# Local scores on TensorE: the products with the queries' high part first, for three groups, and one semaphore each for high and low transposes

## The reference, cut to what matters

```python
q = rmsnorm(apply_partial_rope(h @ Wq_c @ Wq_up))            # per head
k_sw = rmsnorm(apply_partial_rope(h @ Wk)); v_sw = h @ Wv    # one key head
ck = rmsnorm(h.reshape(b, nb, M * HID) @ W_comp)             # 64 blocks of 16 tokens
c_out = attend(einsum(q, ck) * scale, blocks that ended before the token, sink, ck)
s = einsum(q, k_sw) * scale
sw_out = attend(CAP * tanh(s / CAP), the last 64 tokens, sink, v_sw)
inter = einsum('btgf,gfi->btgi', c_out + sw_out, Wg)         # 4 groups
x = layernorm(x + inter @ Wo)
x = layernorm(x + x @ ternary(weight).T + bias)
```

## Time and profile before

| | |
|---|---|
| median of 3 runs | 408.3 us (404.14, 408.30, 408.51) |
| the profiled execution's own time | 405.67 us |
| its span, first to last instruction | 403.9 us |
| mean granted TensorE clock | 0.974 |
| TensorE busy | 364.0 us (90%) |
| VectorE, ScalarE, GpSimd busy | 328.0, 293.3, 280.6 us |
| a step from one tile's local scores to the next | 18.2 to 20.4 us |

### The profile page before, as it was taken

The page is one execution under the profiler, slowest core; times in us unless marked ns, Lnnn a source line. Parts: engine busy times, 40 slices in busy tenths (PEclk is TensorE's granted clock), DMA queues, the critical chain, the costliest instruction groups (busy, mean ns, idle before and its releaser), DMA issues. The chain is left out here.

```text
span 403.9 us, 8848 instructions
## 1 busy us (share of the span) xinstructions
PE 364.0 (90%) x3111; PEld 294.8 (73%) x3111; DVE 328.0 (81%) x676; ACT 293.3 (73%) x833; POOL 280.6 (69%) x197
## 2 busy tenths in 40 slices
PE   6998899779988989999999999988999999989881
PEld 5996678566767778786869787867686868677871
DVE  3688988577989899898989897989898989892524
ACT  4669747768696969797969695978879696958410
POOL 1860155456787888889887977797979797885812
PEclk9999699959999999999999999999999999999997
DMA  8994005498867676758585968686668876676350
GB/s 255 289 268 159 1 0 106 209 262 130 125 98 127 97 132 93 144 80 145 85 152 70 147 98 139 86 145 105 119 120 117 131 116 123 104 127 105 52 86 26
DMA packets 150284, 50.21 MB, mean 124 GB/s; under 512 B 138592, under 2 KB 148832, under 8 KB 149984
## 3 DMA queue, kind: packets, MB, share of 16 engines
q1 hardware_dynamic: 149424, 49.32, 65.3%
q10 hardware_dynamic: 816, 0.33, 0.3%
HBM read 11.87 MB, written 4.19 MB: 40 GB/s over the span
## 5 line engine op out<-in xcount | busy, mean ns | idle before, releaser
L1326 POOL TENSOR_TENSOR room_wg<-room_comp,keep 128x1024 f32<-128x1024 f32 x32 | 75.4, 2355 | 38.4 <-ACT room_comp L868 33.5
L1316 POOL TENSOR_TENSOR ao<-room_wg,ao 128x1024 f16<-128x1024 f32 x31 | 66.2, 2136 | 13.9 <-ACT ao L727 13.8
L687 PE MATMUL PS<-V,room_wg 128*128 128x129 f32 x512 | 67.2, 286 | 5.5 <-POOL room_wg L1326 5.0
L880 ACT ACTIVATE room_h<-PS,room_K 128x8 f32<-128x8 f32 (+7 forms) x256 | 70.8, 392 | 0.5 <-DVE room_K L1129 0.4
L687 PEld LDWEIGHTS PS<-V,room_wg 128*128 128x128 f32 x512 | 62.3, 198 | 9.9 <-POOL room_wg L1326 8.7
L880 ACT ACTIVATION_READ_ACCUMULATOR room_h<-PS,room_K 128x1 f32 x256 | 65.5, 278 | 0.0
L647 PE MATMUL PS<-Weff,aoT 128*128 128x256 f16 x512 | 60.8, 273 | 3.1 <-DMA aoT<-ao 3.0
L1333 POOL TENSOR_TENSOR ny<-nx,nu 128x16 f32<-128x16 f32 x16 | 46.8, 2923 | 20.6 <-DVE o_inv L1095 13.2
L647 PEld LDWEIGHTS PS<-Weff,aoT 128*128 128x128 f16 x512 | 49.6, 98 | 11.7 <-DMA aoT<-ao 5.0
L603 PE MATMUL PS<-room_h,kT 128*128 128x512 f16 x192 | 47.0, 380 | 11.6 <-DMA room_h<-room_K 10.4
L1044 DVE TENSOR_REDUCE ssq<-room_wg 128x8 f32<-128x1024 f32 x30 | 36.5, 1220 | 14.4 <-ACT room_wg L785 14.0
(11 more groups left out here) (186 smaller groups left out, 726.1 us busy)
## 6 DMA issues: line engine op xcount, KB each, us to landing
H<-in_L_attn_h SPq DMA_DIRECT2D x4, 512.0 KB, 6.2
room_wg<-in_L_attn_Wg SPq DMA_DIRECT2D x1, 2048.0 KB, 16.3
cw_rows<-staged SPq DMA_DIRECT2D x1, 2048.0 KB, 6.9
CW<-cw_rows SPq DMA_DIRECT2D x1, 2048.0 KB, 8.0
aoT<-ao SPq DMA_TRANSPOSE x128, 2.7
out<-room_wo SPq DMA_DIRECT2D x16, 128.0 KB, 2.1
CW<-in_L_attn_Wq_up SPq DMA_DIRECT2D x2, 512.0 KB, 9.6
room_wo<-in_L_attn_Wo SPq DMA_DIRECT2D x1, 1024.0 KB, 18.0
```

The lines of the kernel that those rows point to most:

```text
L687: last = nc.tensor.matmul(pv, Pm[:, c, 2 * pr:2 * pr + 2, :], V[:, 2 * i + c, :], start=True, stop=True)
L880: last = nc.scalar.activation(Ec[:, 0:n, hd], bank(4 + hd // 8)[:, (hd % 8) * n:(hd % 8 + 1) * n], ACT.Exp, bias=mn[:, hd:hd + 1], accum_o ...
L1316: G.tensor_tensor(ao16[:, 1, c, :, :], ao[:, c, :, :], ao16[:, 0, c, :, :], ALU.subtract).then_inc(g_al, 1)
L1326: G.tensor_tensor(Pm[:, c, :, :], E[:, c, :, :], keep[:, :, :], ALU.mult).then_inc(g_mask, 1)
```

## The change

For the groups 0 to 2 the products with the queries' high part are all made first (six products, two per group), then the three with the low part; group 3 follows with its three products as before. The high transposes now count on `s_qh` and the low ones on `s_ql`, 32 per tile each. TensorE waits for `s_qh` before the first product and for `s_ql` before the seventh. `norm_T` stands behind the low product of group 1. The two other waits on `s_qt` (ScalarE before it writes a high part again, VectorE before it writes a low part again) now name the semaphore of their own part; each still waits for the tile before. The order in which SyncE issues is the same.

```diff
-                                 transpose=True).then_inc(s_qt, 16)
+                                 transpose=True).then_inc(s_qh if n == 0 else s_ql, 16)
...
-                    pe.wait_ge(s_qt, 64 * i + 64)
                     at = i * P + (i // TPB) * WIN
-                    for u, b in enumerate((6, 4, 5, 6)):
-                        wait(pe, *((a_tanh, 4 * i + 1) if u == 3 else (d_ao, 2 * i)))
+
+                    def local_scores(u, parts):
+
                         c, hf = divmod(u, 2)
-                        for n, (kp, qp) in enumerate(PARTS):
-                            last = nc.tensor.matmul(bank(b), kT[:, kp, at + c * WIN:at + c * WIN + P],
+                        for kp, qp in parts:
+                            last = nc.tensor.matmul(bank((6, 4, 5, 6)[u]), kT[:, kp, at + c * WIN:at + c * WIN + P],
                                                     qT[:, qp, 8 * hf:8 * hf + 8, c * WIN:(c + 1) * WIN],
-                                                    start=n == 0, stop=n == 2)
-                        last.then_inc(p_sw, 1)
+                                                    start=kp == qp == 0, stop=qp == 1)
+                        return last
+
+                    pe.wait_ge(s_qh, 32 * i + 32)
+                    wait(pe, d_ao, 2 * i)
+                    for u in range(3):
+                        local_scores(u, PARTS[:2])
+                    pe.wait_ge(s_ql, 32 * i + 32)
+                    for u in range(3):
+                        local_scores(u, PARTS[2:]).then_inc(p_sw, 1)
                         if ffn and u == 1:
                             norm_T()
+                    pe.wait_ge(a_tanh, 4 * i + 1)
+                    local_scores(3, PARTS).then_inc(p_sw, 1)
...
-                wait(act, s_qt, 64 * t - 48 + 16 * hf)
+                wait(act, s_qh, 32 * t - 16 + 16 * hf)
...
-                    wait(dve, s_qt, 64 * i + 48 + 16 * hf)
+                    wait(dve, s_ql, 32 * i + 16 + 16 * hf)
```

More of the change, by code:

```diff
@@ L210, in build @@
             "g_mask", "g_cn", "g_al", "g_rl", "g_x1", "g_xb", "g_sh"))
-        s_out, s_qt, s_ah, s_al = sem("s_out"), sem("s_qt"), sem("s_ah"), sem("s_al")
+        s_out, s_qh, s_ql, s_ah, s_al = sem("s_out"), sem("s_qh"), sem("s_ql"), sem("s_ah"), sem("s_al")
         s_chain = sem("s_chain")
```

## The result

| | before | changed |
|---|---|---|
| median | 406.58 us (403.4 to 408.88, 20 runs) | 404.92 us (402.94 to 406.78, 20 runs) |
| profiled execution, its span | 405.67, 403.9 us | 406.64, 404.8 us |

The ratio is 0.995 with an interval of 0.9927 to 0.9972: the changed kernel is faster by some 2 us (1.1 to 3.0), where +0.3 us was forecast. The time lies within the forecast range, but it moved by more than its uncertainty, and not in the direction forecast. Two repeats gave 0.9962 (0.993 to 0.9995) and 0.9958 (0.9924 to 0.9992). Every ratio here leaves out the few runs that lie over 1.5% above the fastest of their kernel. The profiled execution of the change is longer than that of before, 406.64 against 405.67 us. This says already that one trace against one trace can't tell where the 2 us are.

A forecast was written before the change was run, and what follows sets the result against it. TensorE is busiest (90%), but ScalarE's row of work from the division's end was taken to set each step. Terms: +0.68 + 0.26 - 0.66 = +0.3 us on the median of 408.3, giving 408.6 us; range 404.0 to 411.0.

The forecast's parts named there:

- The wait removed: Before the local scores: TensorE starts at the division's end, saving 0.42 of 1.09 us of waiting in step 10.
- the first group: Group 0 is released after seven products instead of three: 1.79 us from first product to tanh, before 0.92.
- steps 1 to 6 and 9 to 14: Tanh 1.87 us behind the division, 0.08 us to spare; TensorE's gain is waited out at group 3: worth zero.
- Rival A: TensorE's gain at the front of the steps is passed on: 4.9 us faster, 403.4 us; chance 0.11.
- rival B: Tanh of group 0 in twelve steps lacks the 0.08 us to spare: 1.6 us more, 410.2 us; chance 0.2.
- Steps 7 and 8: TensorE arrives last, ScalarE waits 0.15 and 0.28 us; with step 6's 0.04, less 0.21 absorbed: +0.26 us.
- Step 0: ScalarE already waits for the scores; tanh 0.87 us later, 0.19 absorbed in a later wait: +0.68 us to the end.
- Step 15: No new queries; products start at the division's end, so everything to the last tile's output comes earlier: -0.66 us.
- Rival C: Half clock after step 0's longer idle time lasts into step 1's products: +3.65 us, 412.3 us; chance 0.04.
- the four products: Four more products before group 0's release: 0.217 us each from the trace; the skill's 131 ns would make 0.52 us.
- The upper bound of +1.7 us: The sum if the first group's full 0.87 us delay counts in steps 0, 7 and 8, which have no long wait.

The follow-up runs named there:

- `middle`: New order of products in steps 3 to 14 alone, old order elsewhere, against the kernel before: ratio 0.9997 (0.9969 to 1.0025).
- the filled kernels: Five spare products ahead of step 15's scores: in the old order, ratio 0.9972, repeated 0.998; with the new order in step 15 alone, 0.9983, all against the kernel before.
- `old`: The kernel before, unchanged, run once more against itself: ratio 1.0018 (0.9978 to 1.0059).
- `old4`: The kernel before, unchanged, run again for one more trace; no ratio given, 39.11 us from the first local scores to the tanh of step 2.
- `early`: New order of products in steps 0 to 2 alone, old order elsewhere, against the kernel before: ratio 0.9988 (0.9954 to 1.0021).
- `last2`: New order in step 15 alone, first repeat, against the kernel before: ratio 0.9975 (0.9939 to 1.0011).

## Why the prediction was wrong

*The wait removed, the first group, steps 1 to 6 and 9 to 14: right.* TensorE starts at the division's end, the tanh stands 1.88 us behind, steps 3 to 14 keep their length, `middle` is 0.9997. Rival A (-4.9 us) and rival B are out: ScalarE waits for the scores only 3 times in the run, 3.0 us in all. These are steps 0 (1.97 us), 1 (0.21) and 15 (0.82); I had listed 0, 7 and 8. The zero for these steps holds for a trace with landings in time; with a late one in step 12 the new order saves some 0.7 us, which I did not price.

*Steps 7 and 8, +0.26 us: right in place, not carried to the end.* In step 8 the tanh follows the products by 232.75 - 230.97 = 1.78 us (before 1.51) and the step is 20.55 us long (20.30); step 9 is 19.64 instead of 19.88. All of the quarter is given back, where I had taken 0.21 back. No wait is printed, the delay is only in the tanh's distance. Step 7 does not get longer (19.99 us from tanh to tanh, before 19.98).

*Step 0, +0.68 us: failed. It alone gave the forecast its wrong sign; without it the sum is 0.26 - 0.66 = -0.4 us.* ScalarE's wait grew from 1.11 to 1.97 us, as forecast. But I carried it to the end because the mask and the value products hang on it, and did not follow it into step 1. There the scores wait for transposes that end late anyway (0.84 us in before), and the delay is gone.

*Step 15, -0.66 us: right for the chain (0.68), and the main miss.* I priced the 2.51 us of idle time as idle time only and put what the clock does behind it at nothing. The trace I read had the clock full there, and I took this for a property of the kernel. It was one of three such traces in seven. In the other four the clock fell and the end came 1.9 us later, and with the changed order it fell in none. Rival C had the right mechanism, but I looked for it only where the change lengthens an idle time, not where it shortens one.

The account, from the start of ScalarE's copy in step 15 to the end of the span, landings not delayed: 42.72 us in the four old-order traces with a fall, 40.98 in the three without, 40.36 in the seven of the new order. So the chain gives 0.6 us, a fall costs 1.7, and 4 of 7 make this 1.0: together 1.6 us, against 2.0, 1.5 and 1.7 us by the three ratios. The count of 4 in 7 is small; with 2 to 6 in 7 the clock's share would be 0.5 to 1.5 us. That the fall belongs to the long idle time is shown by traces and mean clocks; the timing of the filled kernels agrees but would not carry it alone. Why an execution with this idle time is hit or spared stays open. The median of 404.92 us lies in the forecast range because that is 7 us wide; the account behind it was another.

*Two sums of the forecast are off.* With 0.52 us for the four products its own terms give 0.52 - 0.19 - 0.66 = -0.33 us, not -0.2. The upper bound of +1.7 us holds only with the 0.21 us of step 8 taken back; the full delay three times gives 3 x 0.87 - 0.66 = +1.95.

## What to carry to other kernels

When a change shortens or lengthens a time in which TensorE stands idle, price what the clock may do behind it, in both directions, also when the trace at hand shows it full: count it over several executions. The same goes for how late a transfer lands. A delay must be followed until it meets a wait that ends late anyway; only what passes that is carried to the end. Filling idle time to hold the clock can move the fall to a place where it costs more.

## What the runs showed of the hardware

The granted clock is not the same from one execution of a kernel to the next: around step 15 of one and the same program it was full in one trace and half (0.52) in three others. Its level after a wait of about 2.2 to 2.8 us went either way; behind waits of 1.8 us and less in that place it never fell in twelve traces. The same holds for the landing of a transposing DMA: the slowest of tile 12 took 3.3 us in nine traces and 4.7 to 5.1 us in nine. In four of these nine (`old`, `old4`, `early`, `last2`) the store issued behind the transposes took 1.40 to 1.45 us of SyncE's row instead of 0.58; which of the two delays the other is not shown. Two plain DMAs of some 128 KB take 1.06 us of SyncE's row.
